# Three rotating PSUM work banks in place of four in a two-layer transformer kernel

## The chip, the cores and the metric

The kernel runs on one core of one Trainium2 chip. The metric is the device time of one execution in microseconds (us), as the median of several runs. Before the change it is 1803.69 us (three runs, 1802.77 to 1805.55).

## What is computed

Sixteen sequences of 256 tokens with 512 features go through two blocks that are conditioned on a vector per sequence. The first block is an attention with 16 heads of 32 features, keys and values from a latent of 128, and a sparse mask; the second an attention with 8 heads of 64 features over one key and value head, then a gated MLP of 2048.

```
x = x + softmax(rope(q) rope(k)^T / sqrt(32) + sparse mask) v Wo      q, k, v from adaptive layernorm of x
x = x + softmax(rope(q) rope(k)^T / sqrt(64)) v Wo                    q, k, v from adaptive RMS norm of x
out = x + (silu(h Wg^T) * (h Wu^T)) Wd^T                              h = adaptive RMS norm of x
```

Sparse mask of the first block: blocks of 128 tokens see no later block; inside, a query sees keys at most 64 away, and every 64th key.

## The kernel before

**Rounds and engines.** The sequences are worked in eight rounds of two (`PAIR`); s is the sequence in the pair, t one of its two tiles of 128 tokens. Every engine has one fixed, hand-ordered list of instructions, and semaphores join the lists. Rounds are overlapped: while attention of round m runs, TensorE (PE) fills the time between its pieces with the MLP of round m-1. The tables `PLAN` and `FIRST_PARTS` deal the parts of that MLP (six matmuls each) to the steps of the round in front of them. The first round has no MLP beside it; the last MLP runs alone at the end.

**fp16 in halves.** Every fp32 operand is split into a high and a low fp16 half, and each product is three matmuls (L1427, L1428, L1429). So ScalarE (ACT) writes a high half from PSUM, then VectorE (DVE) reads the same bank and writes the low half; DVE is the last reader of nearly every bank.

**The eight PSUM banks.** Four `work_bank`s, two `ybank`s (query projections and attention outputs), one `gate` and one `up` bank for the MLP. `ORDER` lists the 76 uses of the work banks in a round: transposes of the normalised input (`fill0`), latents (`lat`), keys and values (`kv`, `near`), attention units (`unit0`, `unit1`), transposes of attention outputs (`heads0`, `heads1`), output projections (`out0`, `out1`), and so on. Use number m of the round takes bank m modulo `BANKS`. `before(n, use)` (L228) finds the use that had this bank last, `last_read` (L106) the semaphore of that use's last reader, and `bank_for` (L1437) makes PE wait for it:

```
def bank_for(n, *name):
    use = USE[name]
    m, last = before(n, use)
    key, per, k = last_read(ORDER[last])
    need(pe, events[key], count(m, per, k))
    return work_bank[use % BANKS]
```

**An attention unit.** Layer 0 has 24 units in a round (four heads by 128 keys in units 0 to 7, two heads by 193 keys in units 8 to 23), layer 1 has 16 (two heads by 256 keys). Unit j passes through:

1. PE: scores into a work bank (`unit_scores`, L1498 in layer 0, L1503 and L1505 in layer 1; in the first round layer 0 adds the mask by a matmul, L1491)
2. DVE: row minima, and the mask in layer 0 (`lows`, L1102, L1106)
3. ACT: exponentials in place with their sums (`exps`, L864)
4. ACT: high half into `prob` (`prob_highs`, L873), which has three slots
5. DVE: low half into `prob` (`prob_lows`, L1113); it frees the bank with semaphore `prob_split`
6. SyncE: a transposing DMA of both halves to `prob_t`
7. PE: product with the values into a `ybank` (`unit_values`)

**The order of the steps.** In step j PE works the MLP parts that are dealt to the step, then the scores of unit j+2 (`AHEAD` is 2), then in some steps a `heads` transpose (L1462), then the values of unit j-4 (`LAG` is 4). DVE works in step j the gates and inner products of the MLP parts of this step (`between`: L1382, L1392), then `prob_lows(j)`, then `lows(j+2)`, then the low half of a `heads` transpose. ACT works `prob_highs(j)`, the tanh of a gate, `exps(j+1)`, the high half of a `heads` transpose, the high half of an inner product. `FILL_AT` puts `heads0` of sequence 0 and 1 behind the scores of steps 20 and 22, and `heads1` at steps 12 and 14, so the order of uses near the end of a layer's attention is unit 22, heads of s=0, unit 23, heads of s=1 (in layer 1: unit 14, heads, unit 15, heads). The second halves of the `heads` and the four output projections follow.

Of the kernel before, what the change touches and what calls it, by code (L numbers as in the profile page):

```python
# [7 lines left out]
ALU = mybir.AluOpType  # L8
# [7 lines left out]
P = 128  # L16
# [34 lines left out]
    [(s, t, [(2 * k + j, j * TOK, TOK) for j in range(2)])  # L51
     for t in range(TILES) for k in range(4) for s in BOTH]]
UNITS = [len(units) for units in UNIT]
BANKS = 4

AHEAD, LAG = 2, 4
FIRST_OF = [{(s, t): min(j for j, (s_, t_, _) in enumerate(units) if (s_, t_) == (s, t))
# [25 lines left out]
         + [("out1", s, 1) for s in BOTH] + [("fill4", s, b) for s in BOTH for b in range(2)])  # L83
USE = {name: m for m, name in enumerate(ORDER)}
USES = len(ORDER)
assert USES % BANKS == 0

HI_ORDER = ([("fill0", s, b) for s in BOTH for b in range(2)]
            + [name for layer in range(2) for name in (
# [12 lines left out]
def unit_index(layer, j):  # L102
    return layer * UNITS[0] + j
# [95 lines left out]
def count(n, per, k):  # L199
    i, off = n  # L200
    return off * per + k if i is None else i * per + (off * per + k)


def need(eng, sem, value):
    if isinstance(value, int) and value <= 0:
        return
    eng.wait_ge(sem, value)


def need_apart(eng, sem, value, met):  # L210
    if isinstance(value, int):
        need(eng, sem, value)
        return
    value = eng.to_reg(value)
    eng.wait_ge(*met)
    eng.wait_ge(sem, value)


def at_start(n):
    return n[0] is None and n[1] == 0  # L220
# [5 lines left out]


def before(n, use):  # L228
    return (n, use - BANKS) if use >= BANKS else ((n[0], n[1] - 1), use - BANKS + USES)


def build(nc, x, cond_t, pos_t, w_ada_t, b_ada_t, wq0_t, wkd_t, wku_t, wvu_t, wo0_t, ln1_w, tw1_t,
          ln2_w, tw2_t, wq1_t, wk1_t, wv1_t, wo1_t, wg_t, wu_t, wd_t, mask_c, rope0_c, freq_c,
          wgu, out):
    with ExitStack() as ctx:
        def sb(name, shape, dt=F32):
            return ctx.enter_context(nc.sbuf_tensor(name, shape, dt))
# [41 lines left out]

        SLOTS, TURNED = 3, LAG + 1
        prob = sb("prob", [P, SLOTS, 2, 512], F16)
        prob_t = sb("prob_t", [P, TURNED - 1, 2, 4, P], F16)
        low = sb("low", [P, BANKS, 4])
        sums0 = sb("sums0", [P, PAIR, TILES, H0])
        sums1 = sums0[:, :, :, 0:H1]
        inv = sb("inv", [P, PAIR, TILES, H0])
# [28 lines left out]
        def bank(name):  # L317
            return ctx.enter_context(nc.psum_tensor(name, [P, 512], F32))

        work_bank = [bank(f"bank{m}") for m in range(BANKS)]  # L320
        ybank = [bank("y0"), bank("y1")]
# [509 lines left out]
        def _(act):  # L831
            def fill(n, f, s):
                for b in range(2):
# [3 lines left out]
                    for c in (2 * b, 2 * b + 1):  # L837
                        src = work_bank[use % BANKS][:, (c % 2) * TOK:(c % 2 + 1) * TOK]
                        if f == 0:
# [10 lines left out]
            def heads(n, layer, s, t):  # L850
                use = USE[f"heads{layer}", s, t]
                need(act, full, count(n, USES, use + 1))
                act.activation(act_t[s][0][:, :, t * P:(t + 1) * P],
                               work_bank[use % BANKS][:].rearrange("p (c q) -> p c q", c=CH),
                               ACT.Copy).then_inc(hi_done, 1)

            def exps(n, layer, j):
                done = unit_index(layer, j) + 1
                need(act, low_ready, count(n, sum(UNITS), done))
                bank_ = work_bank[USE[f"unit{layer}", j] % BANKS]  # L860
                s, t, columns = UNIT[layer][j]
                for k, (h, at, wid) in enumerate(columns):
                    total = (sums0 if layer == 0 else sums1)[:, s, t, h:h + 1]
                    ins = act.activation(bank_[:, at:at + wid], bank_[:, at:at + wid], ACT.Exp,  # L864
                                         bias=low[:, j % BANKS, k:k + 1], scale=-1.0,
                                         accum_out=total)
                ins.then_inc(terms_made, 1)

# [8 lines left out]
            def layers(n, m, first=False):  # L877
# [21 lines left out]
                def units(layer):  # L899
                    total = UNITS[layer]  # L900
                    ahead(f"scores{layer}")
                    exps(n, layer, 0)
                    behind(f"scores{layer}")
                    for j in range(total):
                        prob_highs(n, layer, j)
                        ahead(f"unit{layer}_{j}")
                        if j + 1 < total:
                            exps(n, layer, j + 1)
                        if j in FILL_AT[layer]:
                            heads(n, layer, FILL_AT[layer][j], 0)  # L910
                        behind(f"unit{layer}_{j}")
# [149 lines left out]
        def _(dve):  # L1061
# [29 lines left out]
            def lows(n, layer, j):  # L1091
                use = USE[f"unit{layer}", j]
                need_apart(dve, full, count(n, USES, use + 1), (const_in, 32))
                bank_ = work_bank[use % BANKS]
                if layer == 0 and at_start(n):
                    heads, wid = len(UNIT[0][j][2]), UNIT[0][j][2][0][2]
                    ins = dve.tensor_reduce(low[:, j % BANKS, 0:heads], bank_[:].rearrange(
                        "p (h k) -> p h k", h=heads)[:, :, 0:wid], AX.X, ALU.min)
                elif layer == 0:
                    for k, (h, at, wid) in enumerate(UNIT[0][j][2]):  # L1100
                        view = bank_[:, at:at + wid]
                        ins = dve.tensor_tensor_reduce(  # L1102
                            out=view, in0=view, in1=mask[:, 0:wid], scale=1.0, scalar=3.0e38,
                            op0=ALU.add, op1=ALU.min, accum_out=low[:, j % BANKS, k:k + 1])
                else:
                    ins = dve.tensor_reduce(low[:, j % BANKS, 0:2], bank_[:].rearrange(  # L1106
                        "p (h k) -> p h k", h=2), AX.X, ALU.min)
                ins.then_inc(low_ready, 1)

# [25 lines left out]
            def units(n, m, layer):  # L1135
                total = UNITS[layer]
                between(m, f"scores{layer}")
                lows(n, layer, 0)
                lows(n, layer, 1)
                for j in range(total):  # L1140
                    step = f"unit{layer}_{j}"
                    between(m, step)
                    if step in LN_STATS:
                        ln_stats((n[0], n[1] + 1), LN_STATS[step])
                    elif step in LN_APPLY:
                        ln_apply((n[0], n[1] + 1), LN_APPLY[step])
                    prob_lows(n, layer, j)
                    if j + 2 < total:
                        lows(n, layer, j + 2)
                    if j in FILL_AT[layer]:  # L1150
                        heads_low(n, layer, FILL_AT[layer][j], 0)
                    if j in NORM_AT[layer]:
                        normalise(n, layer, NORM_AT[layer][j], 0)
# [271 lines left out]
        def _(pe):  # L1425
# [11 lines left out]
# [6 lines that stand above are left out]
# [364 lines left out]
```

## Time and profile before

| what | value |
|---|---|
| median of three runs | 1803.69 us |
| profiled execution: span from its first to its last instruction | 1804.9 us |
| runs, one by one | 1805.55, 1803.69, 1802.77 us |
| PE busy | 1717.2 us, 95% |
| DVE busy | 1152.3 us, 64% |
| ACT busy | 945.9 us, 52% |
| POOL busy | 398.8 us, 22% |
| packets moved by DMA | 234.30 MB |

The profiled execution has no other time of its own than its span, which lies inside the range of the runs. In the costliest groups of the page stand the MLP's matmuls (L1427 to L1429 into `gate` and `up`, some 380 ns each where they overlap). A steady round takes 210 us: `work` of the second sequence's rotation stands in the chain of waits at 673.86, 885.48, 1095.12, 1305.10 and 1515.26 us. In the round that is read most closely below, the fifth, attention of layer 0 runs from about 889 to 953 us and that of layer 1 from 990 to 1024 us.

### The profile page before, as it was taken

What the parts mean: (1) busy time and instruction counts of PE and PEld (TensorE: products, weight loads), DVE (VectorE), ACT (ScalarE), POOL (GpSimd) and SP (SyncE); (2) the same over time, 40 slices, a digit from 0 to 9 for tenths busy, and PEclk for the clock granted to TensorE, in tenths of its full rate; (3) what the DMA queues carried; (4) which work ended last, traced back from release to release, by engine and by line L of the source; (5) the groups of instructions that cost most, each with busy time, mean ns of one, the idle gap of its engine ahead of it and who ended that gap; (6) DMA issues with size and microseconds to landing.
All of it is one profiled execution on the core that took longest, in us unless ns stands there. A gap on an engine that the chain in (4) does not pass through costs nothing.

```text
span 1804.9 us, 37773 instructions
## 1 busy us (share of the span) xinstructions
PE 1717.2 (95%) x12440; PEld 931.9 (52%) x12440; DVE 1152.3 (64%) x2858; ACT 945.9 (52%) x2769; POOL 398.8 (22%) x556
## 2 busy tenths in 40 slices
PE   6686899999999999999999999999999999999999
PEld 2344445555455545555455554555455554555444
DVE  6759566675667657685576756676576855767320
ACT  3836456364664538564483646645385644835320
POOL 3438587011111112111110111111121111101120
PEclk9676999999999999999999999999999999999999
DMA  7866489462784449662593637944485725936220
GB/s 245 152 181 115 126 197 253 98 117 82 163 175 94 80 119 184 133 118 78 127 194 91 119 88 161 171 95 82 115 192 125 123 73 138 196 85 112 100 70 24
DMA packets 527231, 234.30 MB, mean 130 GB/s; under 512 B 476336, under 2 KB 493744, under 8 KB 527024
## 3 DMA queue, kind: packets, MB, share of 16 engines
q1 hardware_dynamic: 511472, 175.09, 48.9%
q10 hardware_dynamic: 15552, 56.63, 10.1%
q8 instruction: 108, 1.77, 0.4%
q14 instruction: 99, 0.81, 0.2%
HBM read 90.09 MB, written 16.78 MB: 59 GB/s over the span
## 4 chain that ended last, share of the span: by engine, by line
PE 77%; DVE 10%; DMA 6%; issue 4%; ACT 2%; SPq 1%; DVEq 0%; POOL 0%; ACTq 0%
PE up L1427 8%; PE up L1429 8%; PE up L1428 8%; PE gate L1427 7%; PE gate L1429 7%; PE gate L1428 7%; PE y L1427 4%; PE y L1428 4%; PE y L1429 4%; PE bank L1427 4%; PE bank L1429 4%; PE bank L1428 4%; DMA prob_t<-prob 3%; PE bank L1454 2%; DVE prob L1113 2%
## 5 line engine op out<-in xcount | busy, mean ns | idle before, releaser
L864 ACT ACTIVATE bank<-bank,low 128x128 f32<-128x128 f32 (+2 forms) x768 | 302.7, 395 | 68.2 <-DVE low L1106 35.0
L702 POOL TENSOR_TENSOR inner_t<-inner,inner_t 128x512 f16<-128x512 f32 x128 | 149.0, 1164 | 662.7 <-ACT inner_t L1045 662.6
L1113 DVE TENSOR_TENSOR prob<-bank,prob 128x512 f16<-128x512 f32 (+1 forms) x320 | 202.8, 634 | 54.3 <-ACT prob L873 53.4
L873 ACT ACTIVATE prob<-bank 128x512 f16<-128x512 f32 (+1 forms) x320 | 178.7, 558 | 73.3 <-DMA prob_t<-prob 44.5
L1427 PE MATMUL up<-mlp,ring 128*128 128x512 f16 x512 | 194.9, 381 | 12.8 <-DVE inner L1392 12.8
L1382 DVE SCALAR_TENSOR_TENSOR silu<-silu,gate 128x512 f32<-128x512 f32 x128 | 87.9, 687 | 183.8 <-ACT silu L1039 183.0
L1427 PE MATMUL gate<-mlp,ring 128*128 128x512 f16 x512 | 194.0, 379 | 1.4 <-DVE mlp L1078 0.9
L1429 PE MATMUL up<-mlp,ring 128*128 128x512 f16 x512 | 194.9, 381 | 0.0
L1428 PE MATMUL up<-mlp,ring 128*128 128x512 f16 x512 | 194.9, 381 | 0.0
L1429 PE MATMUL gate<-mlp,ring 128*128 128x512 f16 x512 | 194.0, 379 | 0.0
L1428 PE MATMUL gate<-mlp,ring 128*128 128x512 f16 x512 | 193.9, 379 | 0.0
L864 ACT ACTIVATION_READ_ACCUMULATOR bank<-bank,low 128x1 f32 x768 | 157.0, 204 | 0.0
L1392 DVE SCALAR_TENSOR_TENSOR inner<-up,silu 128x512 f32<-128x512 f32 x128 | 88.3, 690 | 82.3 <-PE up L1429 73.1
L1102 DVE CUSTOM_DVE_ANT_0 bank<-bank,mask 128x128 f32<-128x128 f32 (+1 forms) x448 | 133.2, 351 | 1.4 <-PE bank L1498 1.3
L1039 ACT ACTIVATE silu<-gate 128x512 f32<-128x512 f32 x128 | 76.5, 597 | 105.6 <-PE gate L1429 103.7
L1009 ACT ACTIVATE work<-x_mid 128x512 f32<-128x512 f32 x64 | 40.4, 632 | 171.5 <-DVE x_mid L1173 171.5
L1045 ACT ACTIVATE inner_t<-inner 128x512 f16<-128x512 f32 x128 | 80.9, 632 | 90.3 <-DVE inner L1392 89.3
L1427 PE MATMUL y<-v_hi,prob_t 128*128 128x32 f16 (+2 forms) x1024 | 110.3, 186 | 0.6 <-DMA prob_t<-prob 0.4
L1428 PE MATMUL y<-v_lo,prob_t 128*128 128x32 f16 (+2 forms) x1024 | 109.1, 185 | 0.0
L1429 PE MATMUL y<-v_hi,prob_t 128*128 128x32 f16 (+2 forms) x1024 | 109.1, 185 | 0.0
L1427 PE MATMUL y<-wq_hi,act_hi 128*128 128x512 f16 x256 | 97.1, 379 | 5.7 <-DVE work L1180 4.1
L1427 PE MATMUL bank<-wo_hi,act_hi 128*128 128x512 f16 x256 | 98.5, 385 | 1.3 <-DVE act_lo L1087 1.3
(182 smaller groups left out, 4041.8 us busy)
## 6 DMA issues: line engine op xcount, KB each, us to landing
ring<-wgu_dram ACTq DMA_DIRECT2D x108, 512.0 KB, 3.8
x_in<-x_dram SPq DMA_DIRECT2D x18, 512.0 KB, 3.8
x_res<-x_mid SPq DMA_DIRECT2D x16, 512.0 KB, 3.0
wgu_dram<-ring SPq DMA_DIRECT2D x16, 512.0 KB, 3.6
out_dram<-x_res SPq DMA_DIRECT2D x32, 256.0 KB, 2.3
prob_t<-prob SPq DMA_TRANSPOSE x256, 3.5
inner_t<-wd_t_dram SPq DMA_DIRECT2D x4, 1024.0 KB, 8.7
ring<-wg_t_dram SPq DMA_DIRECT2D x16, 256.0 KB, 4.1
```

Of the source, the lines that this page charges most:

```text
L702: pool.tensor_tensor(inner_t[:, 1, f, :], inner[:], inner_t[:, 0, f, :], ALU.subtract).then_inc(inner_low, 1)
L864: ins = act.activation(bank_[:, at:at + wid], bank_[:, at:at + wid], ACT.Exp, bias=low[:, j % BANKS, k:k + 1], scale=-1.0, accum_out=total)
L873: act.activation(terms(prob[:, g % SLOTS, 0, :], layer, j), terms(work_bank[USE[f"unit{layer}", j] % BANKS][:], layer, j), ACT.Copy).then_ ...
L1039: act.activation(silu[:], gbank[:], ACT.Tanh, scale=0.5 / WS).then_inc(tanh_done, 1)
L1045: act.activation(inner_t[:, 0, f, :], inner[:], ACT.Copy).then_inc(inner_high, 1)
L1102: ins = dve.tensor_tensor_reduce(out=view, in0=view, in1=mask[:, 0:wid], scale=1.0, scalar=3.0e38, op0=ALU.add, op1=ALU.min, accum_out=low ...
L1113: dve.tensor_tensor(terms(prob[:, slot, 1, :], layer, j), terms(work_bank[USE[name] % BANKS][:], layer, j), terms(prob[:, slot, 0, :], lay ...
L1382: dve.scalar_tensor_tensor(silu[:], silu[:], 1.0, gbank[:], ALU.add, ALU.mult).then_inc(gated, 1)
L1392: dve.scalar_tensor_tensor(inner[:], ubank[:], 0.5 * HS / (WS * WS), silu[:], ALU.mult, ALU.mult).then_inc(inner_ready, 1)
L1427: pe.matmul(out_ap, left[0], right[0], start=start, stop=False)
L1428: pe.matmul(out_ap, left[0], right[1], start=False, stop=False)
L1429: return pe.matmul(out_ap, left[1], right[0], start=False, stop=stop)
```

## The change

`BANKS` goes from 4 to 3. The tensors `bank0` to `bank2` stay, and the eighth PSUM bank is not allocated. The 76 uses of a round are no multiple of three, so each round starts again with bank 0, and `before` finds the last use of that bank in the round before. `low`, the buffer of row minima that was indexed by `BANKS`, keeps its four places under a name of its own.

```diff
-BANKS = 4
+BANKS = 3
...
-assert USES % BANKS == 0
+PLACES = -(-USES // BANKS) * BANKS
...
 def before(n, use):
-    return (n, use - BANKS) if use >= BANKS else ((n[0], n[1] - 1), use - BANKS + USES)
+    if use >= BANKS:
+        return n, use - BANKS
+    last = use - BANKS + PLACES
+    return (n[0], n[1] - 1), last if last < USES else last - BANKS
...
-        SLOTS, TURNED = 3, LAG + 1
+        SLOTS, TURNED, LOWS = 3, LAG + 1, 4
...
-        low = sb("low", [P, BANKS, 4])
+        low = sb("low", [P, LOWS, 4])
...
-                                         bias=low[:, j % BANKS, k:k + 1], scale=-1.0,
+                                         bias=low[:, j % LOWS, k:k + 1], scale=-1.0,
...
-                    ins = dve.tensor_tensor_reduce(
...
-                            op0=ALU.add, op1=ALU.min, accum_out=low[:, j % BANKS, k:k + 1])
+                            op0=ALU.add, op1=ALU.min, accum_out=low[:, j % LOWS, k:k + 1])
```

No engine gets another computing instruction, and none moves in its list. What differs is which bank an instruction names and which value of which semaphore PE waits for ahead of a use.

## Rows read from the trace of the kernel before

**Rows 1.** The page: busy time of two engines, and the granted clock in 40 slices.

```profile
PE 1717.2 (95%) x12440; PEld 931.9 (52%) x12440; DVE 1152.3 (64%) x2858; ACT 945.9 (52%) x2769; POOL 398.8 (22%) x556
...
PEclk9676999999999999999999999999999999999999
```

**Rows 2.** Waits of PE from 600 to 1650 us: waiter, releaser, total us, times, longest.

```profile
PE up L1427 <- DVE inner L1392: 7.3, 5, 1.5
...
PE bank L1462 <- DVE prob L1113: 1.9, 5, 0.6
```

**Rows 3.** Windows, fifth round: length; busy PE, PEld, DVE, ACT, POOL; clock, DMA.

```profile
889.00:953.00 64.00, 62.54 (x558) 34.58 (x556) 49.09 (x182) 52.57 (x179) 12.30 (x11) 1.00 0.96 192
990.00:1024.00 34.00, 33.78 (x322) 21.15 (x321) 29.93 (x55) 26.08 (x83) 7.84 (x18) 1.00 0.84 141
```

**Rows 4.** Timeline, PE, layer 0: scores of units 16 and 23, heads of s=1.

```profile
930.71 0.33 PE L1498 MATMUL bank<-k_t,q_t 96*128 96x193 f16 x2
...
947.38 0.33 PE L1498 MATMUL bank<-k_t,q_t 96*128 96x193 f16 x2
...
950.44 0.60 PE L1462 MATMUL bank<-ident,work 128*128 128x128 f32 x4
```

**Rows 5.** Timeline, DVE, layer 0: low halves of units 13, 21, 22, with MLP work ahead.

```profile
931.04 0.55 DVE L1113 TENSOR_TENSOR prob<-bank,prob 128x386 f16<-128x386 f32 x1
...
948.22 0.69 DVE L1382 SCALAR_TENSOR_TENSOR silu<-silu,gate 128x512 f32<-128x512 f32 x1 [0.92 <-ACT silu L1039]
948.83 0.56 DVE L1113 TENSOR_TENSOR prob<-bank,prob 128x386 f16<-128x386 f32 x1
...
950.64 0.69 DVE L1392 SCALAR_TENSOR_TENSOR inner<-up,silu 128x512 f32<-128x512 f32 x1 [0.61 <-PE up L1429]
951.25 0.55 DVE L1113 TENSOR_TENSOR prob<-bank,prob 128x386 f16<-128x386 f32 x1
```

**Rows 6.** Timeline, PE, layer 1: scores of 8, 11; heads s=0; scores 15; heads s=1.

```profile
1002.60 0.27 PE L1503 MATMUL bank<-k_t,q_t 128*128 128x256 f16 x1
...
1010.13 0.27 PE L1503 MATMUL bank<-k_t,q_t 128*128 128x256 f16 x1
...
1017.20 0.65 PE L1462 MATMUL bank<-ident,work 128*128 128x128 f32 x4 [0.22 <-DVE prob L1113]
...
1019.33 0.27 PE L1503 MATMUL bank<-k_t,q_t 128*128 128x256 f16 x1
...
1021.41 0.60 PE L1462 MATMUL bank<-ident,work 128*128 128x128 f32 x4
```

**Rows 7.** Timeline, DVE, layer 1: low halves of units 5, 8, 12, 13 and 14.

```profile
1004.24 0.69 DVE L1113 TENSOR_TENSOR prob<-bank,prob 128x512 f16<-128x512 f32 x1
...
1011.03 0.69 DVE L1113 TENSOR_TENSOR prob<-bank,prob 128x512 f16<-128x512 f32 x1 [1.38 <-ACT prob L873]
...
1018.41 0.68 DVE L1113 TENSOR_TENSOR prob<-bank,prob 128x512 f16<-128x512 f32 x1
...
1020.21 0.68 DVE L1113 TENSOR_TENSOR prob<-bank,prob 128x512 f16<-128x512 f32 x1
...
1022.22 0.68 DVE L1113 TENSOR_TENSOR prob<-bank,prob 128x512 f16<-128x512 f32 x1
```

**Rows 8.** Timeline, fourth round: PE's scores of unit 18, DVE's low half of unit 15.

```profile
723.90 0.33 PE L1498 MATMUL bank<-k_t,q_t 96*128 96x193 f16 x2
...
725.56 0.56 DVE L1113 TENSOR_TENSOR prob<-bank,prob 128x386 f16<-128x386 f32 x1
```

**Rows 9.** Waits of PE from 45 to 103 us, layer 0 of the first round.

```profile
PE bank L1491 <- DVE prob L1113: 8.0, 12, 1.2
```

**Rows 10.** Windows of the first two rounds in which PE idles; columns as in rows 3.

```profile
72.40:103.10 30.70, 22.44 (x242) 14.78 (x243) 22.45 (x54) 18.91 (x68) 0.00 (x0) 0.50 0.83 140
246.50:249.90 3.40, 1.37 (x13) 0.73 (x10) 3.40 (x4) 2.72 (x4) 3.40 (x3) 1.00 0.32 96
249.90:256.70 6.80, 5.14 (x13) 1.84 (x14) 4.30 (x19) 3.66 (x12) 2.78 (x4) 0.50 1.01 219
```

More of the change, by code:

```diff
@@ L1096, in lows @@
                     heads, wid = len(UNIT[0][j][2]), UNIT[0][j][2][0][2]
-                    ins = dve.tensor_reduce(low[:, j % BANKS, 0:heads], bank_[:].rearrange(
+                    ins = dve.tensor_reduce(low[:, j % LOWS, 0:heads], bank_[:].rearrange(
                         "p (h k) -> p h k", h=heads)[:, :, 0:wid], AX.X, ALU.min)
@@ L1103, in lows @@
                             out=view, in0=view, in1=mask[:, 0:wid], scale=1.0, scalar=3.0e38,
-                            op0=ALU.add, op1=ALU.min, accum_out=low[:, j % BANKS, k:k + 1])
+                            op0=ALU.add, op1=ALU.min, accum_out=low[:, j % LOWS, k:k + 1])
                 else:
-                    ins = dve.tensor_reduce(low[:, j % BANKS, 0:2], bank_[:].rearrange(
+                    ins = dve.tensor_reduce(low[:, j % LOWS, 0:2], bank_[:].rearrange(
                         "p (h k) -> p h k", h=2), AX.X, ALU.min)
```

## The prediction

> **What bounds the kernel now.** I read the page first: PE is busy 95% of the span, DVE 64%, and the granted clock is down only in the first slices [rows 1]. So in nearly all of the span a delay of PE is a delay of the end, unless PE had idle time to give. Then I read PE's list of waits over five steady rounds: the largest entries are 7.3 us in five waits for an MLP product and 1.9 us in five waits of a heads transpose for a freed bank [rows 2]. That is 1.5 us and 0.4 us in a round of 210 us; PE has almost no slack to lose, and banks cost it almost nothing today. Third, the two attentions of the fifth round by windows: PE busy 62.54 of 64 us with DVE 49.09 and ACT 52.57, and 33.78 of 34 us with DVE 29.93 [rows 3]. The clock is 1.00 in both, its upper level of 2.4 GHz. PE leads there, and the chain behind it (minima, exponentials, high half, low half) is nearly as full: 77 and 82% in layer 0, 88% for DVE in layer 1. A bank is held through that whole chain, so the question is how far PE runs ahead of the low half (L1113) that frees its bank.
>
> **What the change does to each wait.** At step j PE writes the scores of unit j+2. With four banks they take the bank of unit j-2; with three, that of unit j-1. The wait moves one unit closer. Where heads transposes stand between the units it moves onto the step itself: heads of s=0 (step 20, in layer 1 step 12) need the low half of that step's own unit, unit 23 (unit 15) that of unit 21 (13), worked in the same step, and heads of s=1 that of unit 22 (14). No computing instruction, DMA or issue is added, removed or moved past a queue; those edits, and the four places of `low` under another name, cost nothing. Behind PE's new wait stand in its queue the scores or transpose itself, the values of unit j-4 and the next MLP parts; DVE and ACT wait for all three, SyncE for the values before it may turn a later unit.
>
> **The price per place** is the end of the low half that now frees the bank, less the time at which PE starts the use today. If positive, PE stops for it.
>
> Layer 0, fifth round [rows 4, 5]:
> - unit 16 now needs unit 13: 931.04 + 0.55 = 931.59, less 930.71: 0.88 us
> - unit 23 needs unit 21: 948.83 + 0.56 = 949.39, less 947.38: 2.01 us
> - heads s=1 needs unit 22: 951.25 + 0.55 = 951.80, less 950.44: 1.36 us
>
> Five other units and the first heads come out between 0 and 0.4 us, by the same subtraction about 1 us together; the other units keep a margin. Sum 5.3 us.
>
> Layer 1 [rows 6, 7]:
> - unit 8 needs unit 5: 1004.24 + 0.69 = 1004.93, less 1002.60: 2.33 us
> - unit 11 needs unit 8: 1011.03 + 0.69 = 1011.72, less 1010.13: 1.59 us
> - heads s=0 needs unit 12: 1019.09 less 1017.20: 1.89 us
> - unit 15 needs unit 13: 1020.89 less 1019.33: 1.56 us
> - heads s=1 needs unit 14: 1022.90 less 1021.41: 1.49 us
>
> Units 6, 7, 12 and 14 add about 1.5 us. Sum 10.3 us. Outside the attentions the third-last use was read long before, or within a few tenths of the need; I take nothing there.
>
> **How much of it becomes time.** The deficits add up only where the low half itself moves later with PE. Where it is late because DVE or ACT has a backlog, a first stop of PE lets them catch up, and the next deficit is met by the lead already given away.
>
> *Layer 0 follows PE.* Ahead of the low half of unit 21 stands a gate product that DVE idled 0.92 us for, through ACT's tanh of PE's gate part in the same step; ahead of unit 22 an inner product for which it idled 0.61 us, released by PE [rows 5]. PE's own delay moves these, so the 2.01 and 1.36 us are paid in full, every round. I take 5.0 of the 5.3 us.
>
> *Layer 1 follows DVE.* Few MLP products stand between, and DVE is 88% busy. The 2.33 us at unit 8 are paid. That lead then covers 1.59 us at unit 11 and the small ones behind it. At the end heads, unit 15 and heads each wait for a low half of their own step, with the transpose's halves on ACT and DVE between them: a short serial chain again, but entered with a lead of 2.3 us given away. I take a third of 1.89 + 1.56 + 1.49 = 4.94 us, 1.6 us. Layer 1 costs 3.9 us; the bounds are 2.33 (nothing at the tail) and 10.3 us (nothing covered).
>
> A full round costs 5.0 + 3.9 = 8.9 us. Rounds two to eight are full ones: 7 x 8.9 = 62 us. Rounds two and four cost more, since their low halves run later behind PE: in the fourth, unit 18 would wait 725.56 + 0.56 - 723.90 = 2.22 us for unit 15 [rows 8]. I allow one such stop and a little, 5 us, in each: 10 us. In the first round PE waits for low halves already, 8.0 us in twelve waits of layer 0 [rows 9], so DVE and ACT set the pace there and an earlier or later PE changes little; only the serial tails of the two layers count, 3.4 + 1.6 = 5.0 us. Restart of PE after about ten stops a round is an estimate at a few hundredths each: 3 us in all.
>
> Sum: 62 + 10 + 5 + 3 = **80 us**. On the profiled span of 1804.9 us that is 1885; the median of the runs is 1.2 us below the span, so about **1884 us**.
>
> *Bounds.* From below: only the deepest deficit of each attention is paid, 2.01 + 2.33 = 4.3 us a round, 7 x 4.3 = 30 us, 1834 us. From above: every deficit is paid, 5.3 + 10.3 = 15.6 us a round, 7 x 15.6 + 10 + 5 = 124 us, 1928 us.
>
> **Against a rule.** PE already waits 0.22 us at the heads transpose of layer 1 for the fourth bank [rows 6], and nothing there suggests that a bank is to spare. The Trainium skill, TensorE: Matmul & The Clock Gate, section "HAM oscillation — how this bites in real kernels", reports a matmul kernel to which PSUM double-buffering gave no further gain. By that rule a bank less would cost 0 and the time stay at 1804; by the rows it costs 80 us, since this kernel holds a bank through four passes of two engines. I go by the rows.
>
> **Rivals.**
>
> *A. The clock falls as well.* Each tail puts two or three stops of 1 to 2 us within some ten. In the first round PE was busy 22.44 of 30.70 us with such stops and the granted clock was 0.50, 1.2 GHz; in the second round, after a stretch with 1.37 of 3.40 us busy, it stayed at 0.50 for 6.8 us [rows 10]. Half speed for 6.8 us costs up to 3.4 us. One fall per attention: 2 x 7 x 3.4 = 48 us on top, 1932 us. Against it: outside the small value matmuls PE stays busy between the stops, and one stop is at most 2.3 us. It decides from the point where two stops of 2 us stand in one idle stretch.
> The same page, section "A second HAM failure mode: psum-queue depth-cycling", tells of a kernel that cycles through PSUM banks and idles briefly so often that the clock swings between its levels. The rows of the first round agree with it (0.50); no steady round does (1.00).
>
> *B. DVE and ACT catch up everywhere.* They have 15 and 11 us of idle time in layer 0's attention [rows 3]. If PE's first stop empties their backlog there too, only the deepest deficits remain: 1834 us. Against: the idle time ahead of DVE's gate and inner products, released by PE.
>
> *C. Not slower: the fourth bank is not what holds the depth.* `prob` has three slots, so the high half of unit j waits for the transposing DMA of unit j-3. If that already keeps the chain three units deep, the fourth bank only lets PE write scores early that nobody can take, and PE's stops would be paid back as shorter waits for values and MLP products. The price is then 0, 1804 us, or a gain of a few tenths from shorter waits. It decides if PE's waits after the attentions hold at least what the stops take; they hold 1.9 us a round at most [rows 2] against 8.9. That speaks plainly against it.
>
> *D. The change does nothing,* because the wait for the third-last use is already implied by another one. True at fills and projections, false at the units: eight subtractions above are positive. I count it with C.
>
> **Chances.** Forecast (1855 to 1905): 0.60. A or full payment (above 1905): 0.19. B (1825 to 1855): 0.18. C and D: 0.03. A range from 1834, the lower bound, to 1935 leaves out C, D, a third of B and the top of A, somewhat under two in ten. A measurement here tells 0.2%, 3.6 us, from no change: slower 0.97, same 0.02, faster 0.01.
>
> **What would show it.** In the profile after, PE's waits name DVE L1113 (line numbers are three higher) as the releaser of scores and heads transposes, 50 to 120 us in all, where the steady rounds now show 1.9 us. In each steady round unit 23 starts about 2 us after the MLP part ahead of it, heads of s=1 1.4 us, and unit 8 of layer 1 2 us. A steady round takes 218 to 220 us in place of 210. DVE and ACT busy times stay. The granted clock stays at 1.00 in steady rounds; if it falls, it is A. If the round grows by under 5 us, B holds; if layer 1 grows by more than layer 0, the cover that I gave it is wrong. The prediction fails outright if PE's waits for L1113 grow and the span does not.

## The result, and the profile after

| | before | three banks |
|---|---|---|
| median | 1803.37 us (4 runs) | 1899.65 us (4 runs) |
| lowest to highest | 1802.77 to 1805.55 | 1896.25 to 1901.09 |
| ratio, with its 95% interval | 1 | 1.0527 [1.0512, 1.0542] |
| span of the profiled execution | 1804.9 us | 1894.3 us |
| fifth round, from first transpose to first transpose | 209.64 us | 221.97 us |

The kernel became 96 us slower; the forecast was 80, and the measured time lies inside the forecast's range of 1855 to 1905 us. The two traces show 89.4 us of the loss. The profiled execution after is the fastest of its four: its own time is 1896.25 us, 3.4 us below the median and 2.0 us above its span. If the time before stands as far above its span, the profiled execution before took about 1806.9 us (an estimate), 3.5 us above its median; the two offsets make up the rest. The forecast took the median to be 1.2 us below the span; its 1884 us are the median before plus 80 all the same.

The page after, the rows that answer to [rows 1], with one more group:

```profile
PE 1736.7 (92%) x12440; PEld 932.6 (49%) x12440; DVE 1157.6 (61%) x2858; ACT 950.6 (50%) x2769; POOL 398.1 (21%) x556
...
PEclk9786999999999999999999999999999999999999
...
L1109 DVE TENSOR_REDUCE low<-bank 128x2 f32<-128x512 f32 x128 | 87.0, 685 | 28.1 <-PE bank L1508 28.1
```

The instructions are the same in kind and number, DVE and ACT are busy within 5 us of before, and the span is 89 us longer. PE idles 70 us more. Its busy time grew too, by 19.5 us (1736.7 less 1717.2), although it does the same work: an MLP matmul is shown 0.38 us long where the next starts 0.22 us after it, so the last one before a stop counts for more; and the granted clock was at 0.50 for 106 us in all, before for 92. The 19.5 us are not divided between the two. Lines stand three higher than before. PE's five largest waits in the whole span:

```profile
PE bank L1465 <- DVE prob L1116: 34.0, 25, 2.5
PE bank L1506 <- DVE prob L1116: 28.6, 30, 4.4
PE bank L1501 <- DVE prob L1116: 19.5, 21, 1.9
PE up L1430 <- DVE inner L1395: 12.4, 7, 3.7
PE bank L1494 <- DVE prob L1116: 12.1, 13, 1.6
```

and the bank waits of the same four kinds in the trace before:

```profile
PE bank L1503 <- DVE prob L1113: 9.1, 9, 3.5
...
PE bank L1491 <- DVE prob L1113: 8.0, 12, 1.2
...
PE bank L1462 <- DVE prob L1113: 5.3, 10, 1.5
...
PE bank L1498 <- DVE prob L1113: 1.7, 3, 1.1
```

L1465 are the heads transposes, L1506 and L1501 the first score matmuls of a unit in layers 1 and 0, L1494 the mask matmul of the first round. All wait for L1116, the low half that frees the bank. Together they are 94.2 us in 89 waits, and before 24.1 us in 34. That is 70 of the 89 us, and PE's longer busy time is the rest. The wait for the MLP product L1395 is 12.4 us, before 12.8.

PE at the places named in the prediction, fifth round (answers to [rows 4, 6]):

```profile
973.51 0.34 PE L1501 MATMUL bank<-k_t,q_t 96*128 96x193 f16 x2 [0.80 <-DVE prob L1116]
...
992.84 0.34 PE L1501 MATMUL bank<-k_t,q_t 96*128 96x193 f16 x2 [1.89 <-DVE prob L1116]
...
997.33 0.66 PE L1465 MATMUL bank<-ident,work 128*128 128x128 f32 x4 [1.26 <-DVE prob L1116]
...
1052.35 0.28 PE L1506 MATMUL bank<-k_t,q_t 128*128 128x256 f16 x1 [1.73 <-DVE prob L1116]
...
1068.32 0.65 PE L1465 MATMUL bank<-ident,work 128*128 128x128 f32 x4 [1.54 <-DVE prob L1116]
...
1070.99 0.28 PE L1506 MATMUL bank<-k_t,q_t 128*128 128x256 f16 x1 [0.37 <-DVE prob L1116]
...
1074.62 0.55 PE L1465 MATMUL bank<-ident,work 128*128 128x128 f32 x3 [1.38 <-DVE prob L1116]
```

The idle time in brackets counts from the modelled end of the matmul before. The delay is a little larger, 2.06 us for 1.89 at unit 23: it is the growth of the distance between two starts of PE, after less before. In that way unit 16 lost 0.95 us, unit 23 2.06, heads s=1 1.43, unit 8 of layer 1 1.90, its tail 1.34, 0.53 and 1.56. With the small ones the fifth round lost 5.8 us in layer 0, 0.4 us at the last transpose of `fill2` and 5.9 us in layer 1; the start of the next round adds the rest to 12.3 us (221.97 less 209.64). From the starts of the rounds in the two traces, the eight rounds lost 9.3, 8.2, 14.0, 10.3, 12.3, 11.9, 11.9 and 12.1 us.

### The profile page after: what moved, and what is told of

It is laid out like the page before. It is cut to its first block, busy times and chain, and to the rows that moved or that the text cites. A ratio compares the mean times of both kernels' runs of the same rounds, so it can differ in the third digit from the quotient of the medians.

```text
span 1894.3 us, 37803 instructions
## 1 busy us (share of the span) xinstructions
PE 1736.7 (92%) x12440; PEld 932.6 (49%) x12440; DVE 1157.6 (61%) x2858; ACT 950.6 (50%) x2769; POOL 398.1 (21%) x556
## 4 chain that ended last, share of the span: by engine, by line
PE 77%; DVE 10%; issue 6%; ACT 3%; DMA 2%; DVEq 1%; POOL 0%; SPq 0%; ACTq 0%; POOLq 0%
PE gate L1432 8%; PE gate L1430 8%; PE gate L1431 7%; PE up L1430 7%; PE up L1432 7%; PE up L1431 7%; PE bank L1430 4%; PE bank L1431 4%; PE bank L1432 4%; PE y L1430 4%; PE y L1432 4%; PE y L1431 4%; DVE prob L1116 3%; PE bank L1457 2%; PE bank L1465 2%
## 5 line engine op out<-in xcount | busy, mean ns | idle before, releaser
L1116 DVE TENSOR_TENSOR prob<-bank,prob 128x512 f16<-128x512 f32 (+1 forms) x320 | 202.6, 633 | 31.9 <-ACT prob L876 31.0
L1430 PE MATMUL up<-mlp,ring 128*128 128x512 f16 x512 | 195.3, 381 | 12.4 <-DVE inner L1395 12.4
L1430 PE MATMUL gate<-mlp,ring 128*128 128x512 f16 x512 | 194.4, 380 | 0.0
L1395 DVE SCALAR_TENSOR_TENSOR inner<-up,silu 128x512 f32<-128x512 f32 x128 | 88.3, 690 | 97.3 <-PE up L1432 87.8
L1048 ACT ACTIVATE inner_t<-inner 128x512 f16<-128x512 f32 x128 | 80.7, 630 | 91.0 <-DVE inner L1395 90.0
L1430 PE MATMUL y<-v_hi,prob_t 128*128 128x32 f16 (+2 forms) x1024 | 110.4, 186 | 0.0
L1109 DVE TENSOR_REDUCE low<-bank 128x2 f32<-128x512 f32 x128 | 87.0, 685 | 28.1 <-PE bank L1508 28.1
L1430 PE MATMUL y<-wq_hi,act_hi 128*128 128x512 f16 x256 | 97.1, 379 | 5.1 <-DVE work L1183 4.1
```

Source lines behind the costliest of these rows:

```text
L1048: act.activation(inner_t[:, 0, f, :], inner[:], ACT.Copy).then_inc(inner_high, 1)
L1109: ins = dve.tensor_reduce(low[:, j % LOWS, 0:2], bank_[:].rearrange("p (h k) -> p h k", h=2), AX.X, ALU.min)
L1116: dve.tensor_tensor(terms(prob[:, slot, 1, :], layer, j), terms(work_bank[USE[name] % BANKS][:], layer, j), terms(prob[:, slot, 0, :], lay ...
L1395: dve.scalar_tensor_tensor(inner[:], ubank[:], 0.5 * HS / (WS * WS), silu[:], ALU.mult, ALU.mult).then_inc(inner_ready, 1)
L1430: pe.matmul(out_ap, left[0], right[0], start=start, stop=False)
```

## The experiments

All times are medians beside runs of the kernel before on the same chip. Losses per round and per layer come from the starts of the same uses in two traces, as above.

### The wait alone, with four banks

```diff
 def bank_for(n, *name):
     use = USE[name]
     m, last = before(n, use)
     key, per, k = last_read(ORDER[last])
-    need(pe, events[key], count(m, per, k))
+    near, later = before_three(n, use)
+    key3, per3, k3 = last_read(ORDER[later])
+    if key3 != key:
+        need(pe, events[key], count(m, per, k))
+    need(pe, events[key3], count(near, per3, k3))
```

> Four banks stay in rotation, but TensorE waits before each use for the last reader of the third-last use as well, as the changed kernel does. Theory (the whole loss is the earlier wait on the semaphore): 1890 to 1905 us, and the stops of the changed kernel at the same places, 2.1 us at unit 23 and 1.9 us at unit 8 of layer 1. Rival (three banks cost something beyond the wait, such as TensorE, VectorE and ScalarE meeting more often in a bank): clearly under 1885 us, the rest being that cost.

`before_three` finds the third-last use, as the changed kernel's `before` does. Measured: 1900.62 us (1898.82 to 1905.74), ratio 1.0547 [1.0524, 1.0570]; three banks had 1.0527 [1.0512, 1.0542]. Its fifth round lost 5.9 us in layer 0 and 5.9 in layer 1, with three banks 5.8 and 5.9. PE's waits from 900 to 1700 us (L1473 are the heads transposes, L1509 and L1514 the scores of layers 0 and 1):

```profile
PE bank L1473 <- DVE prob L1120: 13.8, 10, 1.5
PE bank L1509 <- DVE prob L1120: 12.8, 15, 1.9
PE bank L1514 <- DVE prob L1120: 7.0, 9, 1.7
```

With three banks the same window has 13.8, 11.7 and 7.0 us. The loss is the earlier wait: which bank is written plays no part that these runs can tell, with intervals of some 0.4%.

### The heads transposes out of the rotation

```diff
-PLACES = -(-USES // BANKS) * BANKS
+TURN = [name for name in ORDER if name[0][:5] != "heads"]
+BANK = [BANKS if name[0][:5] == "heads" else TURN.index(name) % BANKS for name in ORDER]
...
-    if use >= BANKS:
-        return n, use - BANKS
-    last = use - BANKS + PLACES
-    return (n[0], n[1] - 1), last if last < USES else last - BANKS
+    same = [m for m in range(USES) if BANK[m] == BANK[use]]
+    k = same.index(use)
+    return (n, same[k - 1]) if k else ((n[0], n[1] - 1), same[-1])
```

Every `work_bank[... % BANKS]` becomes `work_bank[BANK[...]]`, and a fourth bank is allocated again.

> The units and all else rotate over three banks, the heads transposes have the fourth bank to themselves. Theory (6.9 of the 12.2 us that a steady round lost stand at the places where a use needs the low half of its own step, and these are made by the heads in the rotation; 1.9 and 2.4 us stand at ordinary units of layers 0 and 1): those 6.9 us go, 1840 to 1855 us. Rival (VectorE and ScalarE are behind in any case, and the tail would be waited for at the units ahead of it): the stops move to the units, 1880 us or more.

Measured: 1849.12 us (1847.09 to 1850.64), ratio 1.0256 [1.0239, 1.0274]. Half the loss is gone, and the stops did not move to the units. In the fifth round the same two places of layer 0, unit 23 and the heads of s=1, start with no idle time:

```profile
968.09 0.33 PE L1501 MATMUL bank<-k_t,q_t 96*128 96x193 f16 x2
...
971.14 0.60 PE L1465 MATMUL bank<-ident,work 128*128 128x128 f32 x4
```

The distance of 3.05 us between them is again that of before (950.44 less 947.38, 3.06 us, [rows 4]). Layer 0 lost 2.3 us in place of 5.8, layer 1 2.0 in place of 5.9. The stops at ordinary units stay as they were: 0.95 us at unit 16, 1.90 at unit 8 of layer 1.

### The heads behind the last scores, with three banks and with four

```diff
-FILL_AT = [{20: 0, 22: 1}, {12: 0, 14: 1}]
+FILL_AT = [{22: 0, 23: 1}, {14: 0, 15: 1}]
```

With this order no scores follow a heads transpose before the output projection, so no place is pushed onto its own step.

> Three banks, and the first heads transposes of a layer stand behind all its scores (steps 22 and 23 in layer 0, 14 and 15 in layer 1), so no use needs the low half of its own step any more. Theory (the tail's loss is made by the place of the heads in the rotation, not by the lack of a fourth bank): as with a bank of their own, 1843 to 1860 us. Rival (late heads make the output projections wait for their halves, and it is lost there): 1880 us or more, with waits of the product into bank for L1090.

> Control: four banks, the same late heads. Theory: nothing waits for a bank and little for the halves, 1800 to 1810 us. Rival (late heads cost by themselves): over 1815 us, and so much of the run before is not owed to banks.

Measured: with three banks 1851.43 us (1849.12 to 1851.58), ratio 1.0260 [1.0243, 1.0277]; with four 1802.03 us (1799.53 to 1804.00), 0.9986 [0.9976, 0.9995]. One line gives back half the loss without a fourth bank, and costs nothing with four. PE's waits from 900 to 1650 us, three banks (the wait for the MLP product, 5.8 us as in the changed kernel, left out):

```profile
PE bank L1506 <- DVE prob L1116: 5.9, 6, 1.7
...
PE bank L1430 <- DVE prob L1116: 4.7, 5, 1.0
PE bank L1501 <- DVE prob L1116: 4.2, 8, 0.8
```

L1465 is gone from the head of the list. New is a wait of the first output projection (L1430 into a bank) of up to 1.0 us. The four-bank variant is 1.4 thousandths below the kernel before, in an interval that ends just short of no change; the medians of the kernel before itself differ by 1.5 us between groups of runs (1802.38 to 1803.89), so I call this no gain.

### MLP parts moved to where PE stopped

On top of the late heads:

```diff
-        ("unit1_4", 1), ("unit1_5", 0), ("unit1_6", 0), ("unit1_7", 3), ("unit1_8", 1),
+        ("unit1_4", 1), ("unit1_5", 0), ("unit1_6", 1), ("unit1_7", 2), ("unit1_8", 1),
```

> As the late heads with three banks, and one of the three MLP parts of step 7 of layer 1 goes to step 6, which has none. Theory (units 6 to 8 follow each other with no MLP part between, so unit 8 asks for its bank 1.9 us early; a part of 1.3 us there fills the stop): 1.3 us a round less at unit 8, some 9 us below the late heads alone. Rival (VectorE's backlog is behind it, and the stop moves to the next unit): within 3 us of the late heads alone.

Measured: 1842.04 us (1838.89 to 1843.60), ratio 1.0215 [1.0198, 1.0232], 9.4 us less than without it. PE's waits from 900 to 1650 us show where most of it came from: the longest at a unit of layer 1, that of unit 8, fell from 1.7 to 0.4 us. The 1.3 us were expected; seven rounds of them are 9.1 us.

```profile
PE bank L1506 <- DVE prob L1116: 2.0, 6, 0.4
```

Then the second part as well:

```diff
-("unit0_14", 0), ("unit0_15", 2)
+("unit0_14", 1), ("unit0_15", 1)
```

> As the run before, and one of the two MLP parts of step 15 of layer 0 goes to step 14, which has none. Theory: the 0.95 us at unit 16 go, some 6 us below the run before, about 1835 to 1845 us. Rival (the low half of unit 14 or 15 then stands behind an MLP product that waits for the moved part): within 2 us of the run before, with a stop at units 17 or 18.

Measured: 1837.53 us (1836.12 to 1838.48), ratio 1.0184 [1.0167, 1.0201], 4.5 us less. The waits of layer 0's units in the same window fell from 4.2 us with 0.8 the longest to:

```profile
PE bank L1501 <- DVE prob L1116: 2.1, 7, 0.5
```

In the fifth round the stop at unit 16 is gone and a later one grew from 0.28 to 0.60 us, which fits 4.5 us in place of the expected 6 (0.95 less 0.32, seven times, is 4.4). So of 96 us, 62 came back with the eighth bank still unused, by an order and a dealing that fit three banks. The moved parts were not run with four banks; that they would gain nothing there is not shown, though PE has no stop at units 8 and 16 in the trace before.

### The low half ahead of the MLP product, at every step

```diff
-                    between(m, step)
+                    prob_lows(n, layer, j)
+                    between(m, step)
...
-                    prob_lows(n, layer, j)
```

> Three banks; in each attention step VectorE makes the low half that frees a bank before the gate and inner products of the MLP, not behind them. Theory (in layer 0 the freeing low half is late because it stands behind an MLP product that waits for TensorE's own part of the same step): about 4 of layer 0's 5.8 us a round go, layer 1 stays at 5.9 us, 1865 to 1880 us. Rival (the MLP products are then late instead, and TensorE waits for them): 1895 us or more, with long waits for L1395 or L1385.

> Control to the run before: four banks with the same new order on VectorE. Theory (with four banks the low half is in time either way): within 5 us of 1803. Rival (the later MLP products cost TensorE time by themselves): above 1815 us, and then so much of the run before is owed to them.

Measured: with three banks 1872.00 us (1871.38 to 1873.32), ratio 1.0387 [1.0370, 1.0404]. The time is as expected, the way to it is not: in the fifth round layer 0 lost 4.2 us, where some 1.8 were expected, and layer 1 lost 3.8, where 5.9 were. The two misses cancelled, by luck. In layer 0, 0.85 us of the 4.2 is a new wait for an MLP product. The control missed: 1832.61 us (1826.96 to 1834.09), 1.0156 [1.0135, 1.0176], 30 us slower with four banks. PE's waits from 600 to 1650 us in the control, to be read against [rows 2]:

```profile
PE up L1427 <- DVE inner L1392: 17.9, 16, 1.5
PE bank L1462 <- DVE prob L1113: 4.8, 5, 1.0
```

The product that frees the `up` bank now stands behind a low half for which DVE waits on ACT, and PE waits for it 17.9 us in place of 7.3. Over the whole span DVE waits 130.9 us for the high half, before 53.4, and PE 28.4 us for the MLP product, before 12.8: that is 15.6 of the 27.2 us between the two traces (1832.1 less 1804.9). The heads transposes wait 4.4 us more; the rest is not taken apart. The pair of runs therefore gives no clean price, since the order helps the bank and hurts the MLP.

### The same order in two steps only

```diff
+LOW_FIRST = {"unit0_21", "unit0_22"}
...
+                    if step in LOW_FIRST:
+                        prob_lows(n, layer, j)
                     between(m, step)
...
-                    prob_lows(n, layer, j)
+                    if step not in LOW_FIRST:
+                        prob_lows(n, layer, j)
```

> Three banks, heads in their old place; VectorE makes the low half ahead of the MLP product in steps 21 and 22 of layer 0 alone. In the changed kernel the high half of unit 21 is there 1.3 us before its low half begins, and that of unit 22 3.8 us. Theory (these two stops are the MLP product's, which waits for TensorE's part of the same step): unit 23's stop falls from 2.1 to about 0.8 us and that of the second heads transpose from 1.4 to 0, 2.7 us a round, 1878 to 1885 us. Rival (the high half on ScalarE is what is late, behind the heads' own high half): 1890 us or more.

> Control: four banks, the same two steps. Low-first at every step cost 30 us with four banks, because MLP products came late and TensorE waited for them. Theory (a product is late only where the high half keeps VectorE waiting, not in these two steps, whose high halves are early): within 4 us of 1803. Rival (each step costs about its share, 30 us over 40 steps and seven rounds, with these among the dearest): 1808 us or more.

Measured: three banks 1880.55 us (1877.91 to 1881.72), 1.0422 [1.0403, 1.0441]; four banks 1803.85 us (1800.47 to 1805.30), 1.0003 [0.9993, 1.0013]. Here the control is clean. PE in the fifth round, unit 23 and the heads of s=1:

```profile
984.43 0.34 PE L1505 MATMUL bank<-k_t,q_t 96*128 96x193 f16 x2 [0.60 <-DVE prob L1117]
...
987.50 0.60 PE L1469 MATMUL bank<-ident,work 128*128 128x128 f32 x4
```

and DVE's low half of unit 21, now ahead of the gate product:

```profile
983.81 0.56 DVE L1117 TENSOR_TENSOR prob<-bank,prob 128x386 f16<-128x386 f32 x1 [0.21 <-ACT prob L877]
984.50 0.69 DVE L1389 SCALAR_TENSOR_TENSOR silu<-silu,gate 128x512 f32<-128x512 f32 x1
```

The stop at unit 23 fell to 0.60 us of idle time and that at the heads to none. What is left at unit 23 ends with a low half that waited 0.21 us for ACT's high half. In all, layer 0 lost 3.1 us in place of 5.8, the 2.7 us less that were expected.

## Why the prediction was right, and where its sum was off

**What bounds the kernel.** Right. PE had nothing to give: its waits for banks grew by 70 us, DVE and ACT did the same work, and the span grew by 89.

**One unit closer, and onto the step itself behind the heads.** Right, and shown twice: waits alone reproduce the loss, and taking the heads out of the rotation or behind the scores takes away 51 or 48 us of it.

**The price per place.** The subtraction was right to a tenth where the low half follows PE: 2.01 and 1.36 us forecast at unit 23 and the heads of s=1, 2.06 and 1.43 measured. The difference is the hand-over from the low half's end to PE's start, 0.05 to 0.06 us in 78 of the 89 waits. The prediction left it out of the price per place and had only its term of 3 us for restarts, which stood on no row; thirteen stops a round at 0.06 us are 5.5 us in seven rounds. The MLP product ahead of the low half, named as the cause, is confirmed by the two-step order.

**Layer 0 follows PE: 5.0 of 5.3 us.** It was 5.8. The stops at the ordinary units added up too, with their hand-overs: 0.41, 0.28, 0.95, 0.28 and 0.28 us.

**Layer 1 follows DVE: 3.9 us.** It was 5.9, and this is the step that failed in size. The 2.33 us at unit 8 were right (0.41 at unit 7 and 1.90 at unit 8, with 0.08 at unit 6), and that lead did cover unit 11, whose scores started with 0.87 us to spare. The step that failed is the tail: I took a third of 4.94 us, 1.6, and it was 1.34 + 0.53 + 1.56 = 3.4. I had kept the low halves of units 12 to 14 where they stood. They moved. This is DVE in the tail of layer 1, after:

```profile
1067.51 0.68 DVE L1116 TENSOR_TENSOR prob<-bank,prob 128x512 f16<-128x512 f32 x1
...
1069.64 0.69 DVE L1090 TENSOR_TENSOR act_lo<-bank,act_hi 128x512 f16<-128x512 f32 x1 [0.85 <-ACT act_hi L856]
1070.25 0.68 DVE L1116 TENSOR_TENSOR prob<-bank,prob 128x512 f16<-128x512 f32 x1
1071.70 0.69 DVE L1109 TENSOR_REDUCE low<-bank 128x2 f32<-128x512 f32 x1 [0.77 <-PE bank L1508]
1073.28 0.69 DVE L1403 SCALAR_TENSOR_TENSOR x_res<-gate,x_res 128x512 f32<-128x512 f32 x1 [0.88 <-PE gate L1432]
1073.89 0.68 DVE L1116 TENSOR_TENSOR prob<-bank,prob 128x512 f16<-128x512 f32 x1
```

Measured from the start of this attention, the low halves of units 12, 13 and 14 ended 1.7, 2.7 and 4.3 us later than in [rows 7]. With these ends the price per place comes out right again: heads s=0 lacked 1.89 us, PE came 2.39 us later by the stops at units 6 to 8, and the low half came 1.7 us later, which leaves 1.2 us and the hand-over; measured 1.34. The same sum gives 0.5 us at unit 15 and 1.5 at heads s=1. Between the stop at unit 8 and the low half of unit 12 it was PE's scores that DVE waited for, three times, 0.56 to 0.79 us. In the tail itself, as the rows show, it was also the high half of the heads transpose, which ACT makes from what PE has just written, and a product of the MLP. Over the whole span the minima of layer 1 (L1109 in the page after) stood behind 28.1 us of idle time that PE's scores ended, and before:

```profile
DVE low L1106 <- PE bank L1505: 6.5, 14, 0.6
```

A DVE that was 88% busy [rows 3] had slack of its own once PE was late, and each stop of PE delayed the low half that the next use waited for. The prediction had named this sign: if layer 1 grows by more than layer 0, the cover that it was given is wrong. It grew by 5.9 us against 5.8, and the round took 222 us, not 218 to 220.

**Outside the attentions: nothing.** Nearly: the last transpose of `fill2` waits 0.4 us a round for the low half of the first.

**The ten us for rounds two and four.** Wrong. These rounds lost 8.2 and 10.3 us, less than the other full rounds. The late low halves of the fourth round before (2.22 us at unit 18, [rows 8]) were not there again after; one round's disturbance in one trace was no base for a term. It made up by luck for part of layer 1: rounds two to eight lost 80.7 us in the trace, and 62 + 10 + 3 = 75 were forecast.

**The first round: 5.0 us.** It was 9.3, and neither term was right. The tail of layer 0, for which I took 3.4 us, cost nothing in the end: PE was 3.2 us late at its last heads transpose and level with the trace before at the first scores of layer 1. Layer 1, for which I took 1.6, made PE 3.8 us late at its last heads transpose. Behind it the values and the output projection added 2.5 us: there the clock was at 0.50 until 183.7 us, and in the trace before at 1.00 from 174.8. The last 3.0 us came ahead of the next round's first transposes; the clock was at 0.50 from 200.8 to 207.6 us, and at the same place before at 1.00. PE stood idle there for 1.9 us for which the profile shows no wait, so how much the clock has to do with these 3 us stays open.

**The clock, rival A.** It happened, but small. Before, the clock fell last in the second round, at 249.9 us [rows 10]. After, it fell there twice, at 258.8 and 323.7 us, and once more at 607.0 us, in the third round, where unit 8 of layer 1 stops. Windows around that fall (columns as in [rows 3]):

```profile
603.60:607.00 3.40, 1.44 (x29) 1.14 (x26) 3.38 (x8) 3.05 (x10) 0.59 (x2) 1.00 0.93 154
607.00:610.40 3.40, 3.40 (x22) 1.83 (x21) 1.57 (x3) 2.85 (x10) 2.48 (x8) 0.50 0.70 133
```

PE was busy 1.44 of 3.40 us, and the granted clock was then 1.2 GHz for 3.4 us. That round lost 14.0 us where the fifth to the eighth lost 12; so such a fall costs about 2 us, and it comes in some rounds and not in each. The prediction had put up to 3.4 us on a fall of 6.8; half speed for 3.4 us is 1.7 by the same sum. What was too much was the length and the number of the falls. The prediction let it decide from two stops of 2 us in one idle stretch; here it came with one stop of 1.73 us at unit 8 and a small one before it. The trace of the waits-only kernel has three falls behind its second round, in the third, fourth and seventh rounds, and it is these rounds that lost more than 12.7 us there. Of the five microseconds between the fastest and the slowest run of the changed kernel such falls explain at most two: both runs have a mean granted clock of 0.972, and one fall of 3.4 us takes 0.001 from that mean. Of the waits-only kernel the slowest run (1905.74 us) had 0.969 and the others 0.972 or 0.973 at 1898.82 to 1901.79 us, which is what two to four more falls of 2 us would make. The falls agree with the section "A second HAM failure mode: psum-queue depth-cycling" of TensorE: Matmul & The Clock Gate in the Trainium skill in kind; here it is a fraction of the loss.

**Rivals B, C and D.** B, only the deepest deficit is paid, is refuted by every tail. C, the fourth bank is not what holds the depth, and D, that the wait was implied anyway, are refuted by the 96 us themselves, and the first experiment shows that the wait alone makes them. The report of the Trainium skill, TensorE: Matmul & The Clock Gate, under "HAM oscillation — how this bites in real kernels", of a kernel to which PSUM double-buffering gave nothing does not carry over: 0 by it, 96 us here.

**What stays open.** Why the low half first at every step costs 30 us with four banks is explained for somewhat more than half. The last 34 us of three banks with late heads and two moved parts are 2 to 6 us a round, part of it small stops of 0.1 to 0.5 us at units, and in the first two rounds 11 us that I did not take apart.

## What to carry to other kernels

The price of one buffer less can be read from the trace of the kernel that still has it: for each use, the end of the last reader that will free the buffer, less the time at which the writer starts today. Add these up where the reader follows the writer, and trust a lead that was given away only until the next place where the reader follows the writer again, at the latest where the two are coupled within one step.

A use of another kind that is slipped into a rotation pushes its neighbours one place closer too; such places at each layer's end, five of which stop PE in a full round, made half of this loss, and moving the intruder behind the rotation cost nothing. A table that was dealt for one depth should be dealt again for another before the depth is judged: 62 of 96 us came back that way.

## What the runs showed of the hardware that was not expected

A single short fall of the granted clock to 0.50 for 3.4 us appears in the middle of an otherwise full round, after stops of under 2 us in all in a stretch with PE busy 1.44 of 3.40 us. The same stop in the fifth round, 1.73 us idle at the same unit, left the clock at 1.00. So one stop decides nothing by itself, and the kernel with the waits alone, which stops at the same places, had its falls partly in other rounds. Behind the second round none of the four traces with the waits of four banks has such a fall. Of the eight whose rotation waits for the third-last use, two have none (those with moved parts), three have one, one has two and two have three.
